# Norm of x, its two halves and beta times mask moved to earlier stages of the pass in a gated cross-attention and feed-forward kernel

## The chip, the cores and the metric

The kernel runs on one core of one Trainium2 chip. The metric is the time of one execution on the device, in microseconds. A core has five engines that run beside each other, each through its own list of instructions in order: TensorE (PE, with its weight loads as PEld), VectorE (DVE), ScalarE (ACT), GpSimd (POOL) and SyncE (SP), which here issues DMA transfers. They meet only at semaphores.

## The reference

Sixteen batch elements of x (256 channels x 1024 positions) pass a cross-attention layer and a feed-forward layer. Cut to what matters:

```python
x = x + tanh(g_xattn) * xattn(layernorm(x), ctx, mask, mask_cond, wq, bq, wk, bk, wv, bv, wo, bo, gamma, beta)
x = x + tanh(g_ffn) * ffn(layernorm(x), w1, w3, w2, wr)

def xattn(x, y, mask, mask_cond, ...):          # conv: weights standardised by row, then einsum, + bias, * mask
    q, k, v = conv(y, wq, bq, mask_cond), conv(y, wk, bk, mask_cond), conv(x, wv, bv, mask)   # 8 heads of 32
    scores = softmax(q @ k.T / SCALE)                                # 32 x 32 per head
    out = conv(scores @ v, wo, bo, mask) + x
    out = normalise out over the channels * gamma + beta
    return out * mask

def ffn(x, w1, w3, w2, wr):                      # tokens are the rows of x, 1024 wide
    gates = top-2 softmax gates of x @ wr.T over 8 experts
    h = silu(silu(x @ w1.T) @ w3.T) @ w2.T
    out[expert index] += gate * h                # scatter to the first 8 rows
```

## The kernel before

The kernel takes the batch elements in 8 pairs. Pass j works through the feed-forward layer of pair j and, threaded into it, the attention of pair j + 1. Seven passes carry an attention part: pass 0, which also still lays out the weights w3, and six steady ones. A pass has 16 groups of TensorE work (`GROUPS`), 24 matmuls of 512 columns each; during group g every engine also does stage s = g - 1 of the attention of the next pair. In each group ScalarE takes a tanh from PSUM (L894), VectorE multiplies (L1318), ScalarE makes the f16 high half (L900) and VectorE the low half (L1323). TensorE uses two PSUM banks in turn for this, so group g + 2 waits for L1318 of group g.

"First" and "second" are the two elements of a pair (b = 0 and 1). The stages of the attention, with the lines of the profile:

- stages 0 to 3: projections `project` (L531), evacuated by VectorE's `qk_out` (L1268) and scaled by ScalarE (L840); `scores` (L542) in stages 1 and 3, `softmax` by VectorE (L1183 to L1197) with ScalarE's exponential (L845).
- stages 3 to 5: `out_times_scores` (L554), split by `t1_high` (L856) and `t1_low` (L1273); `times_value` (L571, L576), split by `m_high` (L849) and `m_low` (L1176); ScalarE writes `cb` (L852). The second `out_times_scores` waits for the first `cb`, whose bank it overwrites.
- the norm of x: statistics `ln1` on VectorE (L1161, L1167), coefficients on GpSimd (L348 to L360), `normed` on ScalarE (L790, x scaled by 1024), the high half `x_high` on VectorE (L1172), the low half `x_low` on GpSimd (L375).
- `bias_part` on GpSimd (L410) writes bias times mask to `u`; `bias_tiles` on VectorE (L1206, eight tiles) adds `cb` times mask to it and signals `ub_ready`.
- stages 7 and 8: `long_product` (L591, L595), eight tiles t, which needs both halves of x. VectorE's `attention_out` (L1221, L1225, statistics L1216) takes the tiles up. There are four banks, so from its fifth tile on TensorE waits for L1225 of the tile three back.
- `values` on GpSimd gives the coefficients of the second normalisation (L348 to L360 on `coc`), ScalarE applies them (`v_normed`, L862), and TensorE transposes back in stages 9 and 10 (`attention_back`, L608).
- `add_beta` on GpSimd: beta times mask to `mtmp` (L391), added to x in place (L394), two pairs of instructions a call, four calls a pair of elements, each instruction behind the one before by the semaphore `mtmp_step`.

The order of work is written out by hand: `attention` and `attention_late` of each engine say what stands in which stage. In a group ScalarE and VectorE do the stage's `attention` first, then their part of the feed-forward; ScalarE does `attention_late` behind it.

Of the kernel before, what the change touches and what calls it, by code (L numbers as in the profile page):

```python
# [68 lines left out]
def build(nc, a, out):  # L69
    ctx = ExitStack()  # L70

    def sb(name, shape, dt=F32):
        return ctx.enter_context(nc.sbuf_tensor(name, shape, dt))
# [20 lines left out]
    with ctx:  # L94
# [66 lines left out]
        co = sb("co", [P, 4, 2])  # L161
# [58 lines left out]
        sm = {n: sem(n) for n in names}  # L220
# [106 lines left out]
        def _(pool):  # L327
# [40 lines left out]
            def ln1(q):  # L368
                coefs(q, mv, co, CH, EPS, XS, "ln1", (sm["xs_ready"], q))

            def x_low(q, b):
                pool.wait_ge(sm["xhi_ready"], q + 1)
                for h in range(4):
                    n, at = h // 2, slice(TC * (h % 2), TC * (h % 2) + TC)
                    ins = pool.tensor_tensor(x_lo[:, b, n, at], xs[b][:, n, at], x_hi[:, b, n, at], ALU.subtract)  # L375
                ins.then_inc(sm["xlo_ready"], 1)

            def add_beta(j, b, c):

                q = 2 * j + b  # L380

                for n in (2 * c, 2 * c + 1):
                    h = slice(TC * (n % 2), TC * (n % 2) + TC)
                    if n == 0:
                        pool.wait_ge(mrow_in[b], 16 * (j + 1))
                        pool.wait_ge(sm["xs_ready"], q + 1)
                        pool.wait_ge(sm["gcol_set"], 1)
                        need(pool, sm["xpre_ready"], q)
                    else:
                        pool.wait_ge(sm["mtmp_step"], 7 * q + 2 * n)  # L390
                    pool.tensor_tensor(mtmp[:, :], mrow[:, b, h], gcol[:, 1, c:c + 1].broadcast_to([P, TC]), ALU.mult)\  # L391
                        .then_inc(sm["mtmp_step"], 1)
                    pool.wait_ge(sm["mtmp_step"], 7 * q + 2 * n + 1)
                    pool.tensor_tensor(xa[b][:, c, h], xa[b][:, c, h], mtmp[:, :], ALU.add)\  # L394
                        .then_inc(sm["mtmp_step" if n < 3 else "xpre_ready"], 1)

            def values(q, b):

                coefs(q, mvc, coc, TT, EPS * XS * XS, 1.0, "cn", (sm["v_ready"], TT * q), m1c[:, b, :])
# [5 lines left out]
            def bias_part(q, b):  # L405

                pool.wait_ge(sm["sm_copy"], q + 1)
                for h in range(4):
                    tt = slice(2 * h, 2 * h + 2)
                    ins = pool.tensor_tensor(u[b][:, tt, :], bo_b[:, :].unsqueeze(1).broadcast_to([P, 2, S]),  # L410
                                             m1c[:, b, tt].unsqueeze(2).broadcast_to([P, 2, S]), ALU.mult)
                ins.then_inc(sm["ub_part"], 1)

            def attention(j, s, jn=None):
                if s == 12 and jn is not None:
                    y_largest(jn)
                if s in (3, 4):
                    ln1(2 * j + s - 3)
                if s in (2, 3):
                    bias_part(2 * j + s - 2, s - 2)  # L420
                if s in (5, 6):
                    x_low(2 * j + s - 5, s - 5)
                if s == 7:
                    add_beta(j, 0, 0)
                    values(2 * j, 0)
                    add_beta(j, 0, 1)
                    add_beta(j, 1, 0)
                if s == 8:
                    values(2 * j + 1, 1)
                    add_beta(j, 1, 1)  # L430
                if s in (9, 10):
                    second_norm(2 * j + s - 9)

# [352 lines left out]
        def _(act):  # L786
            def normed(q, b, c_, s_coef, s_done):
                act.wait_ge(s_coef, q + 1)
                for c in range(CH):
                    ins = act.activation(xs[b][:, c, :], xa[b][:, c, :], ACT.Identity,  # L790
                                         bias=c_[:, 3, c:c + 1], scale=c_[:, 2, c:c + 1])
                ins.then_inc(s_done, 1)
# [91 lines left out]
            def attention_late(j, s, jn=None):  # L884

                if s in (13, 14) and jn is not None:
                    y_high(jn, s - 13)
                if s in (4, 5):
                    normed(2 * j + s - 4, s - 4, co, sm["ln1_coef"], sm["xs_ready"])

            def ffn(j, g):
                first = g < FT
# [110 lines left out]
        def _(dve):  # L1003
# [152 lines left out]
            def ln1(j, b):  # L1156
                q = 2 * j + b
                dve.wait_ge(x_in[b], 16 * (j + 1))
                need(dve, sm[("ln2_mv", "ln1_mv")[b]], q)
                for n in range(4):  # L1160
                    ins = dve.bn_stats(bst[:, n, :], xa[b][:, n // 2, TC * (n % 2):TC * (n % 2) + TC])  # L1161
                ins.then_inc(sm["ln1_stat"], 1)
                dve.wait_ge(sm["ln1_stat"], q + 1)
                need(dve, sm["ln1_coef"], q)
                carry()
                for c in range(CH):
                    ins = dve.bn_aggr(mv[:, c, :], bst[:, 2 * c:2 * c + 2, :])  # L1167
                ins.then_inc(sm["ln1_mv"], 1)

            def x_high(q, b):  # L1170
                dve.wait_ge(sm["xs_ready"], q + 1)
                dve.tensor_copy(x_hi[:, b], xs[b]).then_inc(sm["xhi_ready"], 1)  # L1172
# [93 lines left out]
            def qk_out(q, b, t):  # L1266
                dve.wait_ge(sm["qk_mm"], CT * q + t + 1)
                dve.scalar_tensor_tensor(out=qk[b][:, t, :], in0=att[t][:, :], scalar=ysc[:, 2, b:b + 1],  # L1268
                                         in1=qkb_b[:, :], op0=ALU.mult, op1=ALU.add).then_inc(sm["qk_evac"], 1)
# [11 lines left out]
            def attention(j, s):  # L1281
                if s in (0, 2):
                    for t in range(CT):
                        qk_out(2 * j + s // 2, s // 2, t)
                if s in (1, 3):
                    softmax(2 * j + s // 2, s // 2)
                if s == 4:
                    m_low(2 * j, 0)
                if s in (3, 4):
                    t1_low(2 * j + s - 3)  # L1290
                    ln1(j, s - 3)
                if s in (5, 6):
                    bias_tiles(2 * j + s - 5, s - 5)
                    x_high(2 * j + s - 5, s - 5)
                if s == 5:
                    m_low(2 * j + 1, 1)
                if s in (7, 8):
                    attention_out(2 * j + s - 7, s - 7)
                if s in (9, 10):
                    residual(2 * j + s - 9, s - 9)  # L1300
                if s in (11, 12):
                    tokens_low(2 * j + s - 11, s - 11)
# [213 lines left out]
```

## Time and profile before

| | us |
|---|---|
| median of 3 runs (lowest, highest) | 1165.01 (1164.57, 1166.37) |
| profiled execution, its own time | 1164.77 |
| its span in the trace | 1163.0 |
| TensorE busy | 1056.6 (91%) |
| VectorE busy | 806.0 (69%) |
| ScalarE busy | 466.8 (40%) |
| GpSimd busy | 415.6 (36%) |

A "busy" figure is the time in which the engine has at least one instruction in work. Matmuls overlap, so 91% says that TensorE has something to do, and its idle time is what a program can lose there. The steady passes are 127.47 us apart. Positions in the span are in microseconds from its start.

### The profile page before, as it was taken

Reading aid. Unit: us, or ns where it says so; the run is one execution under the profiler, and the core shown is the slowest. Engines: PE = TensorE matmul, PEld = TensorE weight load, DVE = VectorE, ACT = ScalarE, POOL = GpSimd, SP = SyncE. Lnnn points to the kernel's source line nnn. Section 1 sums busy time; section 2 is a strip of 40 time slices with the busy share of each in tenths; the row PEclk is TensorE's granted clock in tenths of the full one; section 3 lists DMA queues with packets and bytes.
Section 4 is the critical chain, followed back from the end, with each engine's and each line's share of the span. In section 5 each row is a group of like instructions: output and inputs, shape, how many; then the busy total and the mean of one; then the engine's idle time right before and its main releaser. Section 6 shows DMA issues by size and latency. Waiting matters only on the chain.

```text
span 1163.0 us, 17830 instructions
## 1 busy us (share of the span) xinstructions
PE 1056.6 (91%) x6627; PEld 608.0 (52%) x6627; DVE 806.0 (69%) x1913; ACT 466.8 (40%) x714; POOL 415.6 (36%) x500
## 2 busy tenths in 40 slices
PE   4566279899999999999999999999999999999998
PEld 2355145564556555564556555655556455654452
DVE  6787457896679747986689657975788658973221
ACT  4456333345242633354243533353234524262331
POOL 2472002481147403671158212750167114730000
PEclk9778589999999999999999999999999999999999
DMA  8801700017100540027001620035001700054000
GB/s 269 219 19 55 216 1 1 1 63 188 42 1 27 135 128 0 18 78 192 0 0 36 172 80 0 18 117 153 0 0 72 213 4 0 0 142 149 1 1 2
DMA packets 102753, 81.82 MB, mean 70 GB/s; under 512 B 69342, under 2 KB 87332, under 8 KB 102716
## 3 DMA queue, kind: packets, MB, share of 16 engines
q1 hardware_dynamic: 100656, 79.77, 23.5%
q10 hardware_dynamic: 2060, 1.58, 0.5%
q8 instruction: 21, 0.34, 0.1%
q14 instruction: 16, 0.13, 0.0%
HBM read 47.75 MB, written 16.81 MB: 56 GB/s over the span
## 4 chain that ended last, share of the span: by engine, by line
PE 55%; DVE 23%; POOL 8%; issue 8%; ACT 5%; DMA 1%; ACTq 1%; POOLq 0%; DVEq 0%
PE bank L655 38%; PE bank L531 7%; DVE ub L1206 6%; DVE ub L1225 3%; DVE ub L1221 2%; PE bank L542 2%; POOL xbuf L394 2%; POOL mtmp L391 2%; POOL coc L355 2%; DVE bst L1161 2%; PE bank L554 1%; DVE bst L1216 1%; ACT h_hi L900 1%; DVE act_t L1318 1%; DVE x_hi L1172 1%
## 5 line engine op out<-in xcount | busy, mean ns | idle before, releaser
L655 PE MATMUL bank<-xt_hi,w1b 128*128 128x512 f16 x1024 | 326.7, 381 | 0.0
L655 PE MATMUL bank<-w3b,h_hi 128*128 128x512 f16 x1024 | 304.5, 379 | 0.5 <-DVE act_t L1318 0.5
L655 PE MATMUL bank<-xt_lo,w1b 128*128 128x512 f16 x512 | 194.9, 381 | 0.0
L655 PE MATMUL bank<-w3b,h_lo 128*128 128x512 f16 x512 | 194.0, 379 | 0.0
L894 ACT ACTIVATE act_t<-bank,fs 128x512 f32<-128x512 f32 x128 | 87.1, 680 | 193.8 <-PE bank L655 193.7
L1323 DVE SCALAR_TENSOR_TENSOR h_lo<-act_t,h_hi 128x512 f16<-128x512 f32 x128 | 98.4, 769 | 91.7 <-ACT h_hi L900 91.7
L900 ACT ACTIVATE h_hi<-act_t 128x512 f16<-128x512 f32 x128 | 80.8, 632 | 199.2 <-DVE act_t L1318 199.2
L655 PEld LDWEIGHTS bank<-xt_hi,w1b 128*128 128x128 f16 x1024 | 100.6, 98 | 114.3 <-issue 2.1
L1318 DVE SCALAR_TENSOR_TENSOR act_t<-act_t,bank 128x512 f32<-128x512 f32 x128 | 86.2, 673 | 102.0 <-ACT act_t L894 101.8
L655 PEld LDWEIGHTS bank<-w3b,h_hi 128*128 128x128 f16 x1024 | 98.0, 98 | 76.6 <-DVE act_t L1318 0.5
L410 POOL TENSOR_TENSOR ub<-bo_b,mcur 128x512 f32<-128x512 f32 x64 | 64.6, 1039 | 163.8 <-DVE dg L1183 163.8
L348 POOL TENSOR_TENSOR co<-mv,minus 128x2 f32<-128x2 f32 x32 | 7.2, 226 | 243.5 <-DVE mv L1167 153.5
L375 POOL TENSOR_TENSOR x_lo<-xbuf,x_hi 128x512 f16<-128x512 f32 x64 | 80.4, 1288 | 36.6 <-DVE x_hi L1172 31.8
L531 PE MATMUL bank<-wqk_hi,x_hi 128*128 128x512 f16 x256 | 86.9, 384 | 0.8 <-ACT wo_t L806 0.7
L790 ACT ACTIVATE xbuf<-xbuf,co 128x1024 f32<-128x1024 f32 x64 | 75.8, 1232 | 23.3 <-POOL co L360 23.2
L394 POOL TENSOR_TENSOR xbuf<-xbuf,mtmp 128x512 f32<-128x512 f32 x64 | 81.5, 1273 | 5.0
L655 PEld LDWEIGHTS bank<-w3b,h_lo 128*128 128x128 f16 x512 | 50.0, 98 | 60.4
L655 PEld LDWEIGHTS bank<-xt_lo,w1b 128*128 128x128 f16 x512 | 50.3, 98 | 54.8 <-issue 0.8
L1268 DVE SCALAR_TENSOR_TENSOR ub<-bank,ysc,qkb_b 128x512 f32<-128x512 f32 x64 | 47.1, 748 | 45.6 <-PE bank L531 45.4
L862 ACT ACTIVATE ub<-ub,coc 128x256 f32<-128x256 f32 x128 | 64.8, 591 | 29.0 <-POOL coc L360 29.0
L595 PE MATMUL bank<-m_hi,x_hi 128*128 128x256 f16 x256 | 70.1, 274 | 0.0
L595 PE MATMUL bank<-m_hi,x_lo 128*128 128x256 f16 x256 | 70.1, 274 | 0.0
(200 smaller groups left out, 1814.6 us busy)
## 6 DMA issues: line engine op xcount, KB each, us to landing
xbuf<-in_x_dram SPq DMA_DIRECT2D x16, 1024.0 KB, 8.6
out_dram<-xbuf SPq DMA_DIRECT2D x16, 1024.0 KB, 4.2
x_lo<-in_ctx_dram SPq DMA_DIRECT2D x16, 512.0 KB, 3.5
mrow<-in_mask_dram SPq DMA_DIRECT2D x16, 512.0 KB, 4.3
w1b<-in_w_dram SPq DMA_DIRECT2D x8, 512.0 KB, 7.3
w3b<-in_w_dram SPq DMA_DIRECT2D x8, 512.0 KB, 7.7
xbuf<-in_w_dram SPq DMA_DIRECT2D x1, 4096.0 KB, 13.6
xt_hi<-x_hi SPq DMA_TRANSPOSE x32, 4.1
```

What stands on the lines that cost most here:

```text
L375: ins = pool.tensor_tensor(x_lo[:, b, n, at], xs[b][:, n, at], x_hi[:, b, n, at], ALU.subtract)
L394: pool.tensor_tensor(xa[b][:, c, h], xa[b][:, c, h], mtmp[:, :], ALU.add)\
L531: mm = pe.matmul(att[t][:, :], left[b][:, c, P * t:P * t + P], right[:, c, :], start=n == 0, stop=n == 5)
L595: mm = pe.matmul(bk[:, S:2 * S], left[:, b, c, P * t:P * t + P], right[:, b, c, :], start=n == 0, stop=n == 5)
L655: mm = pe.matmul(bk[:, :], left, right, start=d == 0 and n == 0, stop=d == FT - 1 and n == 2)
L790: ins = act.activation(xs[b][:, c, :], xa[b][:, c, :], ACT.Identity, bias=c_[:, 3, c:c + 1], scale=c_[:, 2, c:c + 1])
L862: act.activation(u[b][:, t, :], u[b][:, t, :], ACT.Identity, bias=coc[:, 3, t:t + 1], scale=coc[:, 2, t:t + 1]).then_inc(sm["v_ready"], 1)
L894: act.activation(act_t[:, g % 2, :], fbk[g % 2][:, :], ACT.Tanh, scale=fs[:, 0:1] if first else fs[:, 1:2]).then_inc(sm["th_ready"], 1)
L900: act.activation(h1_hi[:, g, :] if first else h2_hi[:, g % 3, :], act_t[:, g % 2, :], ACT.Copy, scale=H1S if first else H2S).then_inc(sm[" ...
L1206: ins = dve.scalar_tensor_tensor(out=u[b][:, t, :], in0=cb[:, b, :], scalar=m2c[:, b, t:t + 1], in1=u[b][:, t, :], op0=ALU.mult, op1=ALU.add)
L1318: dve.scalar_tensor_tensor(out=buf, in0=buf, scalar=1.0, in1=fbk[g % 2][:, :], op0=ALU.add, op1=ALU.mult)\
L1323: dve.scalar_tensor_tensor(out=lo, in0=buf, scalar=H1S if first else H2S, in1=hi, op0=ALU.mult, op1=ALU.subtract).then_inc(sm["h_lo"], 1)
```

## The change

All of it is in the order of the stages, for the pairs 1 to 7; no instruction is added or taken away, but two waits of GpSimd are new. In VectorE's list `ln1` moves from stages 3 and 4 to stages 1 and 2 and `x_high` from 5 and 6 to 3 and 4. ScalarE's `normed` moves from the end of stages 4 and 5 to the end of 2 and 3. On GpSimd the first `bias_part` waits for the end of the first softmax (`s_ready`), where it waited for its copy out of PSUM; `x_low` moves to stages 3 and 4 and the second `bias_part` between the two; all four `add_beta` calls come in stages 5 and 6, each pair of them behind `ub_ready` of its element, that is behind `bias_tiles`, and ahead of both `values`.

```diff
@@ gpsimd
             def attention(j, s, jn=None):
                 if s == 12 and jn is not None:
                     y_largest(jn)
-                if s in (3, 4):
-                    ln1(2 * j + s - 3)
-                if s in (2, 3):
-                    bias_part(2 * j + s - 2, s - 2)
+                if s == 2:
+                    pool.wait_ge(sm["s_ready"], 2 * j + 1)
+                    bias_part(2 * j, 0)
+                    ln1(2 * j)
+                if s == 3:
+                    ln1(2 * j + 1)
+                    x_low(2 * j, 0)
+                    bias_part(2 * j + 1, 1)
+                if s == 4:
+                    x_low(2 * j + 1, 1)
                 if s in (5, 6):
-                    x_low(2 * j + s - 5, s - 5)
-                if s == 7:
-                    add_beta(j, 0, 0)
-                    values(2 * j, 0)
-                    add_beta(j, 0, 1)
-                    add_beta(j, 1, 0)
-                if s == 8:
-                    values(2 * j + 1, 1)
-                    add_beta(j, 1, 1)
+                    pool.wait_ge(sm["ub_ready"], 2 * j + s - 4)
+                    add_beta(j, s - 5, 0)
+                    add_beta(j, s - 5, 1)
+                if s in (7, 8):
+                    values(2 * j + s - 7, s - 7)
@@ scalar, attention_late
-                if s in (4, 5):
-                    normed(2 * j + s - 4, s - 4, co, sm["ln1_coef"], sm["xs_ready"])
+                if s in (2, 3):
+                    normed(2 * j + s - 2, s - 2, co, sm["ln1_coef"], sm["xs_ready"])
@@ vector
             def attention(j, s):
                 if s in (0, 2):
                     for t in range(CT):
+                        if s == 2 and t == 2:
+                            ln1(j, 1)
                         qk_out(2 * j + s // 2, s // 2, t)
                 if s in (1, 3):
                     softmax(2 * j + s // 2, s // 2)
+                if s == 1:
+                    ln1(j, 0)
                 if s == 4:
                     m_low(2 * j, 0)
                 if s in (3, 4):
                     t1_low(2 * j + s - 3)
-                    ln1(j, s - 3)
+                    x_high(2 * j + s - 3, s - 3)
                 if s in (5, 6):
                     bias_tiles(2 * j + s - 5, s - 5)
-                    x_high(2 * j + s - 5, s - 5)
```

In the rows of the order a line number behind the change is up to two or five higher than before. On ScalarE the place is the start of stage 3 to the cb of stage 4, before the change (L845 exponential, L856 t1_high, L894 and L900 the feed-forward, L849 m_high, L852 cb, L856 the second t1_high):

```order
L845 ACTIVATE dg<-dg 128x64
L856 ACTIVATE t_hi<-bank 128x512
L893 REGISTER_ALU
L894 ACTIVATE act_t<-bank,fs 128x512
L900 ACTIVATE h_hi<-act_t 128x512
L849 ACTIVATE m_hi<-bank 128x512
L852 ACTIVATE cb<-bank,fs 128x256
L856 ACTIVATE t_hi<-bank 128x512
```

And the same place in the changed kernel:

```order
L847 ACTIVATE dg<-dg 128x64
L858 ACTIVATE t_hi<-bank 128x512
L895 REGISTER_ALU
L896 ACTIVATE act_t<-bank,fs 128x512
L902 ACTIVATE h_hi<-act_t 128x512
L792 ACTIVATE xbuf<-xbuf,co 128x1024 x2
L851 ACTIVATE m_hi<-bank 128x512
L854 ACTIVATE cb<-bank,fs 128x256
L858 ACTIVATE t_hi<-bank 128x512
```

The second `normed` now stands between the feed-forward's copy of group 4 and m_high and cb of stage 4; its two instructions stood behind group 5 before.

On GpSimd the place is the list from the first coefficients of a steady pass to the first beta work, as a difference (L410 bias_part, L348 to L360 coefficients, L375 x_low):

```order
-L407 REGISTER_ALU
-L410 TENSOR_TENSOR ub<-bo_b,mcur 128x512 x4
+L345 REGISTER_ALU
 L348 TENSOR_TENSOR co<-mv,minus 128x2
 L349 TENSOR_SCALAR co<-mv 128x2
 L353 TENSOR_TENSOR co<-co,nhalf 128x2
 L360 TENSOR_TENSOR co<-co 128x2
-L375 TENSOR_TENSOR x_lo<-xbuf,x_hi 128x512 x8
+L375 TENSOR_TENSOR x_lo<-xbuf,x_hi 128x512 x4
+L410 TENSOR_TENSOR ub<-bo_b,mcur 128x512 x4
+L375 TENSOR_TENSOR x_lo<-xbuf,x_hi 128x512 x4
```

The second bias_part has moved from in front of the second element's coefficients to between the two halves of x_low.

On VectorE the place is stage 5 to the first tile of attention_out, before (L1206 bias_tiles, L1172 the cast x_high, L1176 m_low):

```order
L1206 SCALAR_TENSOR_TENSOR ub<-cb,mcur,ub 128x256 x8
L1172 CAST x_hi<-xbuf 128x2048
L1176 SCALAR_TENSOR_TENSOR m_lo<-bank,m_hi 128x512
L1317 REGISTER_ALU
L1318 SCALAR_TENSOR_TENSOR act_t<-act_t,bank 128x512
L1323 SCALAR_TENSOR_TENSOR h_lo<-act_t,h_hi 128x512
L1206 SCALAR_TENSOR_TENSOR ub<-cb,mcur,ub 128x256 x8
L1172 CAST x_hi<-xbuf 128x2048
L1317 REGISTER_ALU
L1318 SCALAR_TENSOR_TENSOR act_t<-act_t,bank 128x512
L1323 SCALAR_TENSOR_TENSOR h_lo<-act_t,h_hi 128x512
```

And in the changed kernel:

```order
L1208 SCALAR_TENSOR_TENSOR ub<-cb,mcur,ub 128x256 x8
L1178 SCALAR_TENSOR_TENSOR m_lo<-bank,m_hi 128x512
L1322 REGISTER_ALU
L1323 SCALAR_TENSOR_TENSOR act_t<-act_t,bank 128x512
L1328 SCALAR_TENSOR_TENSOR h_lo<-act_t,h_hi 128x512
L1208 SCALAR_TENSOR_TENSOR ub<-cb,mcur,ub 128x256 x8
L1322 REGISTER_ALU
L1323 SCALAR_TENSOR_TENSOR act_t<-act_t,bank 128x512
L1328 SCALAR_TENSOR_TENSOR h_lo<-act_t,h_hi 128x512
```

Both casts have left this stretch; the rest stands as before.

## Rows read from the trace of the kernel before

**Rows 1.** The page: TensorE's granted clock in tenths of full, 40 slices.

```profile
PEclk9778589999999999999999999999999999999999
```

**Rows 2.** TensorE's waits, 300 to 1100 us: total, times, longest.

```profile
PE bank L591 <- DVE ub L1225: 7.5, 6, 1.2
PE bank L608 <- ACT ub L862: 6.5, 6, 1.1
PE bank L591 <- POOL x_lo L375: 5.0, 6, 0.8
```

**Rows 3.** Timeline of TensorE: start, duration, operation, count, idle before and releaser.

```profile
588.62 1.10 PE L554 MATMUL bank<-wo_t,sblk 128*128 128x256 f32 x4
...
613.02 0.44 PE L591 MATMUL bank<-ident,xbuf 128*128 128x128 f32 x2 [1.24 <-DVE ub L1225]
```

**Rows 4.** Timeline of VectorE, the same pass.

```profile
564.93 2.45 DVE L1197 TENSOR_TENSOR sblk<-dg,dr 32x64 f32<-32x64 f32 x4
...
582.09 0.91 DVE L1197 TENSOR_TENSOR sblk<-dg,dr 32x64 f32<-32x64 f32 x4
...
583.63 2.46 DVE L1161 BATCH_NORM_STATS2 bst<-xbuf 128x6 f32<-128x512 f32 x4
...
595.63 3.25 DVE L1206 SCALAR_TENSOR_TENSOR ub<-cb,mcur,ub 128x256 f32<-128x256 f32 x8
...
603.03 5.05 DVE L1206 SCALAR_TENSOR_TENSOR ub<-cb,mcur,ub 128x256 f32<-128x256 f32 x8
608.00 1.22 DVE L1172 CAST x_hi<-xbuf 128x2048 f16<-128x2048 f32 x1
...
610.51 1.60 DVE L1323 SCALAR_TENSOR_TENSOR h_lo<-act_t,h_hi 128x512 f16<-128x512 f32 x1 [0.70 <-ACT h_hi L900]
612.04 0.41 DVE L1221 TENSOR_TENSOR ub<-ub,bank 128x256 f32<-128x256 f32 x1
...
632.62 0.54 DVE L1232 BATCH_NORM_AGGREGATE mvc<-bst 128x2 f32<-128x6 f32 x7
```

**Rows 5.** Timeline of ScalarE, the same pass.

```profile
588.01 0.47 ACT L852 ACTIVATE cb<-bank,fs 128x256 f32<-128x256 f32 x1
...
594.90 2.36 ACT L790 ACTIVATE xbuf<-xbuf,co 128x1024 f32<-128x1024 f32 x2
...
637.52 4.05 ACT L862 ACTIVATE ub<-ub,coc 128x256 f32<-128x256 f32 x8 [3.12 <-POOL coc L360]
```

**Rows 6.** Timeline of GpSimd, the same pass.

```profile
609.30 4.95 POOL L375 TENSOR_TENSOR x_lo<-xbuf,x_hi 128x512 f16<-128x512 f32 x4 [3.87 <-DVE x_hi L1172]
614.21 1.03 POOL L391 TENSOR_TENSOR mtmp<-mrow,gcol 128x512 f32<-128x512 f32 x1
615.32 1.28 POOL L394 TENSOR_TENSOR xbuf<-xbuf,mtmp 128x512 f32<-128x512 f32 x1
...
634.20 0.21 POOL L348 TENSOR_TENSOR coc<-mvc,minus 128x8 f32<-128x8 f32 x1
```

**Rows 7.** Timelines of VectorE and GpSimd in the prologue.

```profile
59.91 6.06 DVE L1206 SCALAR_TENSOR_TENSOR ub<-cb,mcur,ub 128x256 f32<-128x256 f32 x6
...
60.36 5.33 POOL L375 TENSOR_TENSOR x_lo<-xbuf,x_hi 128x512 f16<-128x512 f32 x4 [4.73 <-ACT x_hi L938]
65.65 1.22 POOL L391 TENSOR_TENSOR mtmp<-mrow,gcol 128x512 f32<-128x512 f32 x1
```

**Rows 8.** TensorE by windows: length, busy time (count), granted clock, DMA share, GB/s.

```profile
49.20:53.00 3.80, 0.02 (x1) 1.00 0.21 51
53.00:55.80 2.80, 0.03 (x1) 0.50 0.00 0
...
151.80:155.40 3.60, 3.60 (x13) 0.50 0.00 0
```

**Rows 9.** The load of x: SyncE's timeline, and the page's us to landing.

```profile
539.51 0.89 SPq L255 DMA_DIRECT2D xbuf<-in_x_dram  x2
...
xbuf<-in_x_dram SPq DMA_DIRECT2D x16, 1024.0 KB, 8.6
```

## The prediction

> **What bounds the kernel now.** I read the page first, then the waits of TensorE, then each engine's timeline over one steady pass, last the clock. The page has TensorE busy for 91% of the span, and its clock is full from the sixth of the 40 slices on [rows 1]. So what is lost later is idle time of TensorE alone. In the waits over the six steady passes three kinds are left [rows 2]: 7.5 us for DVE's tiles of the attention output (L1225), 6.5 us for ScalarE's L862, 5.0 us for GpSimd's low half of x (L375). The reader is to see that this is 19 us, about 3.2 us a pass (4.1 with the issue time around the waits, by the starts of the matmuls), and that no engine other than TensorE is full. I follow the pass that runs from 547.9 to 675.4 us; the others repeat it every 127.47 us. On its timeline TensorE waits 1.24 us up to 613.02 [rows 3], where the fifth tile of stage 7 needs the bank that VectorE's first tile frees; the wait for L862, 1.1 us [rows 2], ends at 639.72. Since DVE starts its first tile at 612.04 [rows 4] and TensorE follows 0.98 us later, **the start of these tiles, D, sets this place**: each microsecond on D is one on the pass.
>
> **Part 1: where D goes.** D is the end of a chain on DVE, and all that the change moves ends in it. Times are those of this pass.
>
> *The norm.* ln1 costs DVE 2.70 us (2.46 for four bn_stats [rows 4], and the aggregation), twice. The first stands now behind the first softmax, whose four products took 2.45 us beside the bias product of GpSimd and 0.91 us without it (the second softmax) [rows 4]; L1188 gains 0.7 too, so 2.2 of 2.7 us come back. The second stands between two evacuations of the second projection and makes the last ready 0.7 us later; the scores of TensorE then wait some 0.3 us. Both are absorbed by what follows. In stages 3 and 4 the norm's place is taken by the cast that makes the high half, 1.22 us. The x that the norm reads is issued at 539.5 and lands 8.6 us later [rows 9]; the norm starts at 565.2, so nothing waits there.
>
> *ScalarE.* The second normed (2.36 us for two L790 [rows 5]) comes now ahead of m_high and L852 in stage 4, before it came behind. ScalarE gets to it at 586.9, is free at 589.1, L852 ends at 590.1 where it ended at 588.48 (588.01 + 0.47 [rows 5]). The product out_times_scores of the second element waits for exactly this; it started at 588.62 [rows 3] and will at 590.2: TensorE is 1.6 us late from here on.
>
> *GpSimd.* x_low of the first element starts when DVE's cast ends, 585.7, and takes 4.95 us for four beside one DVE instruction [rows 6]. bias_part(1) follows from 590.7, is held up by the second cast (1.22 us [rows 4]) and ends at about 595.7. x_low(1) then runs to about 601, which lies over the first bias_tiles of DVE; before it had GpSimd idle beside it, 3.25 us for eight [rows 4].
>
> *How DVE and GpSimd hold each other up.* In the prologue six L1206 take 6.06 us with four L375 beside them [rows 7]: two pass at 0.40, four take 1.30 each, one for each GpSimd instruction. An L375 is 1.12 us without this ((4.95 - 0.45) / 4 [rows 6]), so a product costs GpSimd's instruction less some 0.2 us, plus its own 0.40. The reverse stands in the row of L391, 1.22 us where it has 1.03 alone [rows 6, 7]. In the pass it is seen again: eight L1206 in 5.05 us instead of 3.25, and L1323 in 1.60 instead of 0.69 [rows 4]. The Trainium skill (SBUF — State Buffer, "Who interferes with whom") says that DVE with two SBUF inputs contends with a GpSimd instruction that reads SBUF and that the loser blocks for the whole instruction. The rows agree with the first half and show some 0.2 us less than the second; by the page's wording the six slow products below would be 1.7 us dearer in each pass, by estimate 12 us in all, and I do not use it.
>
> *Sum on DVE.* L1323 of group 6 is issued at 596.0 and ends at 597.3. bias_tiles(0): three slow at 1.30, five at 0.40, 5.9 us, ends at 603.2. m_low(1) 0.6, L1318 0.6, ScalarE's copy 0.7, so the next L1323 is issued at 605.1. But add_beta of the first element begins at 603.2, since it waits for just this ub_ready. L1323 gets through at 606.1. bias_tiles(1) now meets the rest of the eight add_beta instructions, six of them: three L391 at 1.03 - 0.2 + 0.4 = 1.23 and three L394 at 1.28 - 0.2 + 0.4 = 1.48 [rows 6], 8.1 us, and two at 0.40: 8.9 us instead of 5.05, ends at 615.0 (before: 608.1). The cast behind it is gone (-1.14). L1318, the copy and an L1323 that meets the second add_beta take 1.9 to 2.85 us, middle 2.3. **D = 617.3 instead of 612.04: +5.3 us.** L391 and L394 beside several two-input DVE instructions are in no row. The bounds: no wait (0.40 a product) and a wait for every instruction in full, 1.03 or 1.28 and 0.48 for the product; I take the value of the nearest rows, L375's. TensorE is ready for the fifth tile at 612.2 (613.02, less the 1.24 and 1.0 us of waits with the issue time around them, 2.4 us, plus 1.6): it idles 6.1 us.
>
> **Part 2: what is won behind D.** GpSimd had the second coefficients' input at 633.16 but started at 634.20 [rows 4, 6], because the beta work lay in front. In the new order the beta work of both elements (19.8 us) ends at about 625.5, before the first statistics at D + 9.1 = 626.4, so neither element's values are delayed. L862 then starts about 1.2 us earlier (637.52 before [rows 5]), and TensorE's wait of 1.1 us [rows 2], 1.27 with the issue time, and the 0.19 behind it nearly go: -1.25 us. The x_low wait (1.0 us with issue) goes too, but it is inside the 6.1: VectorE's start is late next.
>
> **Part 3: the clock.** The stalls of the steady passes, 1.2 us at the longest [rows 2], leave it full [rows 1]. A stall of 6 us is of another kind: in the prologue TensorE idles from 49.22 to 55.77, and the clock is full for the first 3.8 us and at 0.50 (1.2 GHz of 2.4) after [rows 8]. After the idle time that ends at 151.77 TensorE works without gap, still at 0.50 for 3.6 us [rows 8], and from then on the clock stays full [rows 1]. I take this: 3.6 us at half speed lose 1.8 us. Bounds: 0, and 3.7 us as after 55.77, when the clock came back 7.5 us later, with gaps.
>
> **Sum.** A pass: +5.3 - 1.25 + 1.8 = +5.85 us. Seven passes carry an attention part that the change touches: six steady ones and the first, which has the same stalls plus the w3 weights; its stage 4 has more ScalarE work in front, so I give it the same. 7 x 5.85 = 41 us on the profiled execution's 1164.77 us (0.24 below the median): **1205.7 us**, and with the median 1206. I write 1205.5.
>
> **Rivals.**
> - *Faster: the products do not queue behind the beta work.* L394 is in place and L391 reads a broadcast column; if neither holds DVE, bias_tiles(1) ends at 609.0, D = 610.9, TensorE is at its fifth tile at 612.2 instead of 613.02, and with the 1.25 a pass is 2.05 us shorter: 1165 - 14.4 = 1150.6. It decides from D below 613.3 on. For it: no row has L394 against L1206. Against it: one L391 was lengthened by an L1206 [rows 7], and L410, which also reads a broadcast, held the softmax [rows 4].
> - *The clock holds.* Then +4.05 a pass, 1193.4. For it: TensorE is busy without gap up to the stall, where the prologue's work is thin, and the clock outlasted 3.8 us of idle time even there [rows 8]. Against: the stall forecast is 6.1 us.
> - *Two products to each beta instruction*, because GpSimd waits on its own semaphore between them. bias_tiles(1) ends at 613.0, D = 615.4, idle 4.2 us, +2.1 a pass: 1180, with the clock's loss 1192. Against: in the rows GpSimd gets the next turn each time; its gap between L391 and L394 is under 0.1 us.
> - *The norm does not come early*, because x or GpSimd is late: then about as before. The load's row [rows 9] excludes x.
>
> **Numbers.** The forecast 0.55; clock holds 0.17; two products 0.13; faster 0.09; about nothing 0.03; dearer than 1218 (the page's full block together with a slow return of the clock) 0.03. The range is 1177 to 1218; the likeliest alone has D from 616.8 to 617.8 and 0.9 to 3.1 for the clock, 1196 to 1218. What a measurement can tell from no change is 0.2%, 2.3 us: faster 0.09, same 0.03, slower 0.88.
>
> **What would show it.** The first L1221 of a steady pass some 5 us later in the pass; L1206 at a mean near 1 us (0.603 before), with a total near 15 us a pass for sixteen; TensorE's largest wait L591 for L1225, near 6 us, six times, and none for L375; L862's wait gone; out_times_scores 1.6 us late behind L852; a granted clock below 1.00 just after each long stall. Wrong it would be if bias_tiles(1) stayed near 5 us, if GpSimd were not in add_beta beside it, or if the fifth tile came less than 1.3 us later than before.

## The result, and the profile after

| | before | after |
|---|---|---|
| median of 4 runs, us (lowest, highest) | 1164.87 (1164.57, 1166.37) | 1207.27 (1206.68, 1208.89) |
| ratio to before, with its 95% interval | | 1.0364 [1.0346, 1.0381] |
| profiled execution, its span | 1163.0 | 1205.2 |

The changed kernel is 3.6% slower: the forecast of 1205.5 us is 1.8 us below the median. In the trace a line of before stands two to five lines higher: L1208 is `bias_tiles`, L1328 the feed-forward's low half, L1223 and L1227 the first and third operation of an attention tile, L593 the transposes of `long_product`, L854 `cb`, L864 `v_normed`.

The page, with the clock in 40 slices and the costliest row of `bias_tiles` (busy us, mean ns):

```profile
PEclk9777699999998999899999999899999999899999
...
L1208 DVE SCALAR_TENSOR_TENSOR ub<-cb,mcur,ub 128x256 f32<-128x256 f32 x128 | 110.0, 928 | 0.0
```

The waits of TensorE between 300 and 1100 us (total, times, longest), which answer to [rows 2]:

```profile
PE bank L593 <- DVE ub L1227: 39.6, 6, 6.7
PE bank L556 <- ACT cb L854: 5.2, 6, 0.9
PE bank L544 <- ACT ub L842: 1.2, 6, 0.2
```

The wait for VectorE's tile has grown from 1.2 to 6.7 us a pass, the waits for x_lo and for L864 (then L862) are gone, one for `cb` has come. The clock, full from the seventh slice on before [rows 1], now dips again and again.

I compare one pass with the pass of [rows 3 to 6]. Both are counted from their first matmul of `scores`, which is at 576.19 us here (first row below) and was at 560.03, so this pass stands 16.16 us later in the span. TensorE:

```profile
576.19 1.50 PE L544 MATMUL bank<-ub 128*128 128x128 f32 x12
...
606.34 1.10 PE L556 MATMUL bank<-wo_t,sblk 128*128 128x256 f32 x4 [0.86 <-ACT cb L854]
...
628.06 0.38 PE L657 MATMUL bank<-w3b,h_lo 128*128 128x512 f16 x1
635.09 0.69 PE L593 MATMUL bank<-ident,xbuf 128*128 128x128 f32 x2 [6.65 <-DVE ub L1227]
```

VectorE in the same pass, answering to [rows 4] (start, duration, operation, count, idle before):

```profile
612.17 1.33 DVE L1328 SCALAR_TENSOR_TENSOR h_lo<-act_t,h_hi 128x512 f16<-128x512 f32 x1 [0.70 <-ACT h_hi L902]
613.43 5.94 DVE L1208 SCALAR_TENSOR_TENSOR ub<-cb,mcur,ub 128x256 f32<-128x256 f32 x8
...
621.27 1.37 DVE L1328 SCALAR_TENSOR_TENSOR h_lo<-act_t,h_hi 128x512 f16<-128x512 f32 x1 [0.70 <-ACT h_hi L902]
622.55 8.62 DVE L1208 SCALAR_TENSOR_TENSOR ub<-cb,mcur,ub 128x256 f32<-128x256 f32 x8
631.10 0.68 DVE L1323 SCALAR_TENSOR_TENSOR act_t<-act_t,bank 128x512 f32<-128x512 f32 x1
632.47 1.71 DVE L1328 SCALAR_TENSOR_TENSOR h_lo<-act_t,h_hi 128x512 f16<-128x512 f32 x1 [0.70 <-ACT h_hi L902]
634.11 0.41 DVE L1223 TENSOR_TENSOR ub<-ub,bank 128x256 f32<-128x256 f32 x1
```

And GpSimd, answering to [rows 6]:

```profile
606.83 5.01 POOL L410 TENSOR_TENSOR ub<-bo_b,mcur 128x512 f32<-128x512 f32 x4
611.81 5.31 POOL L375 TENSOR_TENSOR x_lo<-xbuf,x_hi 128x512 f16<-128x512 f32 x4
619.69 1.04 POOL L391 TENSOR_TENSOR mtmp<-mrow,gcol 128x512 f32<-128x512 f32 x1 [2.58 <-DVE ub L1208]
620.81 1.27 POOL L394 TENSOR_TENSOR xbuf<-xbuf,mtmp 128x512 f32<-128x512 f32 x1
...
625.02 1.10 POOL L391 TENSOR_TENSOR mtmp<-mrow,gcol 128x512 f32<-128x512 f32 x1
626.20 1.33 POOL L394 TENSOR_TENSOR xbuf<-xbuf,mtmp 128x512 f32<-128x512 f32 x1
627.60 1.10 POOL L391 TENSOR_TENSOR mtmp<-mrow,gcol 128x512 f32<-128x512 f32 x1
628.78 1.32 POOL L394 TENSOR_TENSOR xbuf<-xbuf,mtmp 128x512 f32<-128x512 f32 x1
...
632.38 1.26 POOL L394 TENSOR_TENSOR xbuf<-xbuf,mtmp 128x512 f32<-128x512 f32 x1
```

Read these two lists side by side. VectorE's first group (613.43 to 619.37) lies over L375; its second (622.55 to 631.17) over the beta work that was released at 619.69; its last L1328 (632.47) over the next L394. Six of eight products in the second group each pay for one GpSimd instruction: from 625.02 on these start 1.18, 1.40 and 1.18 us apart, 1.29 on average for an L391 and an L394, and a held product takes 1.30. The price is nearly all VectorE's: in these rows L391 and L394 take 1.10 and 1.33 us, against 1.03 and 1.28 undisturbed [rows 6]. TensorE stood still from 628.44 to 635.09 meanwhile.

The clock around this stall (length, TensorE busy, granted clock):

```profile
628.40:635.10 6.70, 0.05 (x2) 0.70 0.00 0
635.10:637.90 2.80, 2.80 (x11) 0.50 0.00 0
637.90:641.00 3.10, 3.10 (x24) 0.99 0.00 0
```

TensorE resumes at half speed (1.2 of 2.4 GHz) and gets the full clock back at 637.9. It resumes so after each of the six long stalls; pass 0's stall, 3.65 us, left the clock full.

### The profile page after: what moved, and what is told of

Same layout as the page of the kernel before. It is cut to its first block, busy times and chain, and to the rows that moved or that the text cites. A ratio compares the mean times of both kernels' runs of the same rounds, so it can differ in the third digit from the quotient of the medians.

```text
span 1205.2 us, 17837 instructions
## 1 busy us (share of the span) xinstructions
PE 1069.1 (89%) x6627; PEld 612.7 (51%) x6627; DVE 848.1 (70%) x1913; ACT 467.1 (39%) x714; POOL 415.6 (34%) x500
## 4 chain that ended last, share of the span: by engine, by line
PE 55%; DVE 29%; ACT 8%; issue 7%; DMA 1%; ACTq 1%; POOL 0%; DVEq 0%; POOLq 0%
PE bank L657 36%; DVE ub L1208 9%; PE bank L597 5%; PE bank L533 4%; ACT xbuf L792 3%; DVE bst L1163 3%; DVE act_t L1323 2%; ACT h_hi L902 2%; PE bank L610 2%; PE bank L593 2%; DVE ub L1270 2%; PE bank L544 1%; DVE sblk L1199 1%; PE bank L719 1%; DVE ub L1227 1%
## 5 line engine op out<-in xcount | busy, mean ns | idle before, releaser
L657 PE MATMUL bank<-w3b,h_hi 128*128 128x512 f16 x1024 | 307.7, 382 | 0.5 <-DVE act_t L1323 0.5
L1328 DVE SCALAR_TENSOR_TENSOR h_lo<-act_t,h_hi 128x512 f16<-128x512 f32 x128 | 111.3, 870 | 91.6 <-ACT h_hi L902 91.6
L410 POOL TENSOR_TENSOR ub<-bo_b,mcur 128x512 f32<-128x512 f32 x64 | 70.5, 1131 | 179.6 <-DVE sblk L1199 174.3
L1208 DVE SCALAR_TENSOR_TENSOR ub<-cb,mcur,ub 128x256 f32<-128x256 f32 x128 | 110.0, 928 | 0.0
L593 PE MATMUL bank<-ident,xbuf 128*128 128x128 f32 x256 | 52.8, 290 | 44.5 <-DVE ub L1227 43.9
L375 POOL TENSOR_TENSOR x_lo<-xbuf,x_hi 128x512 f16<-128x512 f32 x64 | 81.4, 1303 | 21.0 <-DVE x_hi L1174 17.2
L394 POOL TENSOR_TENSOR xbuf<-xbuf,mtmp 128x512 f32<-128x512 f32 x64 | 82.4, 1288 | 5.0
L391 POOL TENSOR_TENSOR mtmp<-mrow,gcol 128x512 f32<-128x512 f32 x64 | 72.2, 1129 | 30.4 <-DVE ub L1208 26.7
L657 PEld LDWEIGHTS bank<-xt_lo,w1b 128*128 128x128 f16 x512 | 50.3, 98 | 54.8 <-issue 0.8
L593 PEld LDWEIGHTS bank<-ident,xbuf 128*128 128x128 f32 x256 | 36.9, 150 | 70.9 <-DVE ub L1227 47.9
L864 ACT ACTIVATE ub<-ub,coc 128x256 f32<-128x256 f32 x128 | 64.7, 590 | 20.7 <-POOL coc L360 20.7
```

The costliest lines, as they stand in the source:

```text
L593: pe.transpose(bk[:, P * c:P * c + P], xs[b][:, c, P * t:P * t + P], ident[:, :])
L657: mm = pe.matmul(bk[:, :], left, right, start=d == 0 and n == 0, stop=d == FT - 1 and n == 2)
L1208: ins = dve.scalar_tensor_tensor(out=u[b][:, t, :], in0=cb[:, b, :], scalar=m2c[:, b, t:t + 1], in1=u[b][:, t, :], op0=ALU.mult, op1=ALU.add)
L1328: dve.scalar_tensor_tensor(out=lo, in0=buf, scalar=H1S if first else H2S, in1=hi, op0=ALU.mult, op1=ALU.subtract).then_inc(sm["h_lo"], 1)
```

## The experiments

Each ratio is to the kernel before, measured beside it. "Gap" is TensorE's idle time before the fifth tile of `long_product`; "D" is the start of the first attention tile on VectorE, from the first matmul of `scores`. The mean time between the starts of steady passes, and D and the first and second group of `bias_tiles` in the third of them (the one whose rows are shown):

| kernel | us | ratio [95%] | steady pass | D | groups |
|---|---|---|---|---|---|
| before | 1164.9 | | 127.48 | 52.0 | 3.25, 5.05 |
| after | 1207.3 | 1.0364 | 133.98 | 57.9 | 5.94, 8.62 |
| beta_back | 1180.1 | 1.0128 [1.0111, 1.0145] | 130.03 | 54.4 | 9.54, 3.25 |
| beta_alone | 1214.5 | 1.0419 [1.0401, 1.0436] | 134.29 | 58.1 | 3.25, 10.43 |
| bias_wait | 1165.4 | 0.9999 [0.9990, 1.0009] | 127.47 | 52.0 | 3.25, 5.05 |
| halved | 1186.9 | 1.0185 [1.0168, 1.0202] | 130.97 | 54.8 | 5.94, 6.55 |
| kept_busy | 1226.4 | 1.0527 [1.0506, 1.0548] | 138.43 | 57.9 | 5.95, 8.63 |
| kept_busy2 | 1195.9 | 1.0272 [1.0254, 1.0290] | 131.98 | 57.9 | 5.95, 8.63 |
| cb_first | 1205.5 | 1.0355 [1.0337, 1.0373] | 133.12 | 57.7 | 6.84, 8.62 |
| beta_order | 1158.8 | 0.9945 [0.9929, 0.9962] | 126.21 | 52.0 | 3.25, 5.05 |
| beta_behind | 1150.4 | 0.9877 [0.9861, 0.9894] | 125.10 | 50.8 | 5.94, 3.25 |
| both | 1145.8 | 0.9837 [0.9821, 0.9853] | 124.68 | 50.6 | 6.84, 3.25 |

### beta_back: the changed kernel with the beta work where it was

```diff
-                if s in (5, 6):
-                    pool.wait_ge(sm["ub_ready"], 2 * j + s - 4)
-                    add_beta(j, s - 5, 0)
-                    add_beta(j, s - 5, 1)
-                if s in (7, 8):
-                    values(2 * j + s - 7, s - 7)
+                if s == 7:
+                    add_beta(j, 0, 0)
+                    values(2 * j, 0)
+                    add_beta(j, 0, 1)
+                    add_beta(j, 1, 0)
+                if s == 8:
+                    values(2 * j + 1, 1)
+                    add_beta(j, 1, 1)
```

> The changed kernel with add_beta and values back in stages 7 and 8 as before, all else as changed. If the beta work beside the second bias_tiles is what makes the changed kernel slower (my theory): bias_tiles(1) falls from 8.6 us to 3.3 to 4 us, the first L1221 tile stands near 611 to 612 us of the reference pass instead of 618, the long wait of TensorE for L1227 is under 1 us, the clock stays full, and the time is 1155 to 1163 us, below before. If the cause is the normed ahead of cb on ScalarE (TensorE 1.6 us late), or the norm's place in VectorE's list: most of the loss stays, above 1180 us.

Measured 1180.05 us: most of the loss is gone, and yet the expectation failed. The first `add_beta` has no wait in front; with `x_low` done early it starts beside the first group. VectorE and then GpSimd in the trace of this kernel (`bias_tiles` is L1210):

```profile
603.16 9.54 DVE L1210 SCALAR_TENSOR_TENSOR ub<-cb,mcur,ub 128x256 f32<-128x256 f32 x8
...
615.20 3.25 DVE L1210 SCALAR_TENSOR_TENSOR ub<-cb,mcur,ub 128x256 f32<-128x256 f32 x8
```

```profile
601.54 5.31 POOL L375 TENSOR_TENSOR x_lo<-xbuf,x_hi 128x512 f16<-128x512 f32 x4
606.80 1.22 POOL L391 TENSOR_TENSOR mtmp<-mrow,gcol 128x512 f32<-128x512 f32 x1
608.10 1.33 POOL L394 TENSOR_TENSOR xbuf<-xbuf,mtmp 128x512 f32<-128x512 f32 x1
```

The conflict has changed groups: 9.54 and 3.25 us in place of 5.94 and 8.62. It supports the mechanism and refutes what I took for "undone": the order in the list doesn't keep two engines apart, only a wait or the data does.

### beta_alone: the kernel before with only the beta work moved

```diff
-                if s == 7:
-                    add_beta(j, 0, 0)
-                    values(2 * j, 0)
...
+                if s in (5, 6):
+                    pool.wait_ge(sm["ub_ready"], 2 * j + s - 4)
+                    add_beta(j, s - 5, 0)
+                    add_beta(j, s - 5, 1)
+                if s in (7, 8):
+                    values(2 * j + s - 7, s - 7)
```

> The kernel before with only the beta work and values moved (stages 5 and 6 behind ub_ready, values in 7 and 8). My theory: this part alone brings most of the loss, 1200 to 1225 us, with a wait for L1225 of 5 us or more in each pass and a lowered clock behind it. If the loss needs the earlier norm and the x_low beside the first bias_tiles: 1165 to 1185 us.

Measured 1214.47 us. The longest wait of its TensorE (here L589 is the transposes, L1223 the third operation of a tile):

```profile
PE bank L589 <- DVE ub L1223: 44.1, 6, 7.4
```

This part by itself loses more than the whole change does. Here x_low of the first element still runs when the second group starts, so all eight products are held, two by L375 and six by the beta work: 10.43 us, 8 x 1.30. The slowdown is its work. Of the 7 us more than the changed kernel's, some 2 are in the steady passes and 4.8 in pass 0 (142.7 against 137.9 us), where the clock fell twice.

### bias_wait: the kernel before with only the new wait for the softmax

```diff
+                if s == 2:
+                    pool.wait_ge(sm["s_ready"], 2 * j + 1)
```

> The kernel before with only the first bias product behind the softmax (the wait for s_ready). The softmax of stage 1 takes 3.1 us instead of 5.4. My theory: it is off the path, 1163 to 1166 us, within 0.2% of before. A rival, that VectorE's time in stage 1 counts: 2 us a pass, 1150 us.

Measured 1165.39 us, ratio 0.9999. The softmax did become shorter, 3.1 us instead of 5.4, and the time did not: this wait is off the path.

### halved: the changed kernel with beta instructions of half the length

```diff
-                    pool.tensor_tensor(mtmp[:, :], mrow[:, b, h], gcol[...], ALU.mult)
+                    for m in range(2):   # at, to: 256 columns each
+                        ins = pool.tensor_tensor(mtmp[:, to], mrow[:, b, at], gcol[...], ALU.mult)
...                                          # and the same for the addition to xa
```

> The changed kernel with each of add_beta's two GpSimd instructions per column half (the scalar product and the product with the mask, 512 columns each) cut into two of 256 columns, so that GpSimd does the same work in twice as many instructions. Theory: beside add_beta each two-input VectorE product of bias_tiles waits for one GpSimd instruction, whatever its length; instructions of half the length then hold a product of bias_tiles(1) to some 0.75 to 0.85 us in place of 1.18 and 1.41, its group takes about 6.4 us in place of 8.6, the fifth u tile comes about 2 us earlier and TensorE is idle about 4.4 us before it: 1185 to 1200 us. Rival: a product waits by the total time that GpSimd is at work, so the group keeps its 8.6 us and the kernel its 1207.

Measured 1186.90 us, and this is the sharpest of the tests: GpSimd does the same work in more instructions, and the kernel is 20 us faster than the changed one. Its VectorE (L1213 is `bias_tiles`), then its GpSimd:

```profile
615.36 6.55 DVE L1213 SCALAR_TENSOR_TENSOR ub<-cb,mcur,ub 128x256 f32<-128x256 f32 x8
...
623.20 1.10 DVE L1333 SCALAR_TENSOR_TENSOR h_lo<-act_t,h_hi 128x512 f16<-128x512 f32 x1 [0.70 <-ACT h_hi L907]
```

```profile
616.10 1.43 POOL L393 TENSOR_TENSOR mtmp<-mrow,gcol 128x256 f32<-128x256 f32 x2
617.61 1.65 POOL L399 TENSOR_TENSOR xbuf<-xbuf,mtmp 128x256 f32<-128x256 f32 x2
```

Eight products in 6.55 us are 0.82 us each, and GpSimd passes four instructions from 616.10 to 619.34, 0.81 each: one for one, as with the long ones, where six products take 1.30 us each ((8.62 - 2 x 0.40) / 6). What a product waits for is one instruction of the other engine, whatever its length. D is 3.1 us earlier, the gap 3.6 us instead of 6.7; the clock fell to half after it in the six steady passes too.

### kept_busy and kept_busy2: what the lowered clock costs

In both, the changed kernel's TensorE works through the stall; the products are read by nothing.

```diff
+                if t == 4 and b == 0 and not first_pair(q):
+                    for _ in range(28):      # kept_busy2: range(9), ident and qkb_b, f32
+                        pe.matmul(rbk[:, P:4 * P], wqk_hi[:, 0, 0:P], wqk_hi[:, 0, 0:3 * P], ...)
```

> The changed kernel with 28 added matmuls of 384 columns into an unused part of a bank, issued just ahead of the fifth tile's wait in stage 7 (4.5 us of work inside the idle time of 6.65 us; their result is read by nothing). If the clock's fall behind the long stall costs 1.8 us a pass: granted clock 1.00 all through the passes and 1207 - 6 x 1.8 = 1196 us (1193 to 1199). If the lowered clock costs nothing, because something else sets the time behind the stall: 1207 us. If TensorE's own work were short of time: above 1207.

Measured 1226.37 us, inconclusive on the clock. With the 28 extra products TensorE stopped at the start of five of the passes, 3.3 to 3.9 us each time. Waits of its TensorE, then the queue that carries instructions on its page:

```profile
PE bank L661 <- issue: 18.2, 5, 3.9
```

```profile
q8 instruction: 66, 1.08, 0.4%
```

66 transfers of instructions instead of the 21 on the changed kernel's page, 45 more or nine for each stop. I read this as code that is fetched again because TensorE's program became too long; the profile names the queue, not what the transfers carry. The second version fills the time with fewer instructions.

> The changed kernel with 9 added float32 matmuls of 384 columns (5.9 us of work, read by nothing) ahead of the fifth tile's wait; the 28 of kept_busy made TensorE's loop so long that its code was fetched anew in each pass (66 fetches instead of 21, 3.7 us idle at the loop's start). With 9, if the code stays: 21 fetches, the clock at 1.00 in the passes, and half of 2.85 us saved in each: 1207 - 8.6 = 1199 us. If the lowered clock costs nothing: 1207 us. If the code is fetched anew: 18 to 20 us above one of these.

Measured 1195.90 us, with 21 transfers and the clock full. Its TensorE by windows (length, busy, clock), to be held against the windows above (this pass stands 3.06 us earlier in the span, so its fifth tile starts at 632.03):

```profile
628.40:635.10 6.70, 5.85 (x31) 1.00 0.00 0
635.10:637.90 2.80, 2.80 (x22) 1.00 0.00 0
```

D and both groups are those of the changed kernel, and the fifth tile starts at the same place, 58.90. A pass is 131.98 us instead of 133.98 on average: **the lowered clock costs 2.0 us a pass**, and the stall itself the rest. Pass 0, where the added work is longer than the stall, was 1.5 us longer, so the whole gains 11.4 us and not 12. In single passes of the changed kernel it was 1.4 to 2.9 us (133.36 to 134.92). The longest is the one in which the clock stayed at half for all of this window of the changed kernel:

```profile
768.40:774.50 6.10, 6.06 (x23) 0.50 0.00 0
```

### cb_first: the second norm behind cb on ScalarE

```diff
                     m_high(2 * j + s - 4, s - 4)
+                if s == 4:
+                    normed(2 * j + 1, 1, co, sm["ln1_coef"], sm["xs_ready"])
...
-                if s in (2, 3):
-                    normed(2 * j + s - 2, s - 2, co, sm["ln1_coef"], sm["xs_ready"])
+                if s == 2:
+                    normed(2 * j, 0, co, sm["ln1_coef"], sm["xs_ready"])
```

> The changed kernel with the second normed between m_high with cb and the second t1_high in stage 4. TensorE's wait for cb falls from 0.9 us to under 0.2. My theory: D hangs on VectorE and GpSimd, and moves 0.9 us at most, so 1201 to 1207 us, with a longer idle time before the fifth tile. The rival, that the normed ahead of cb carries the loss: at least 1.2 us a pass less, 1197 us or below.

Measured 1205.45 us. The longest wait of its TensorE:

```profile
PE bank L593 <- DVE ub L1229: 44.9, 6, 7.5
```

The wait for `cb` is gone, and TensorE waits so much longer for VectorE, 7.5 us. TensorE's 1.6 us at `cb` were real and worth nothing there, because the fifth tile sets the time; D moved 0.2 us. A steady pass is 0.86 us shorter all the same, and the rest of that is the clock: it was full again 2.85 us after each stall, in the changed kernel 2.85 to 6.0 us after, 4.0 on average. Pass 0 gives 1.7 us of it back, since its stall grew from 3.65 to 5.23 us and the clock fell there too.

### beta_behind: the beta work behind the last product that it can hold up

```diff
-                if s in (5, 6):
-                    pool.wait_ge(sm["ub_ready"], 2 * j + s - 4)
-                    add_beta(j, s - 5, 0)
-                    add_beta(j, s - 5, 1)
-                if s in (7, 8):
-                    values(2 * j + s - 7, s - 7)
+                if s == 7:
+                    pool.wait_ge(sm["h_lo"], GROUPS * (j - 1) + 8)
+                    add_beta(j, 0, 0)
+                    add_beta(j, 0, 1)
+                    values(2 * j, 0)
+                    add_beta(j, 1, 0)
+                if s == 8:
+                    values(2 * j + 1, 1)
+                    add_beta(j, 1, 1)
```

> The changed kernel with the beta work behind both bias_tiles: it waits for the low half of group 7 (the last instruction ahead of the first tile of attention_out), then add_beta(0,0), add_beta(0,1), values of the first, add_beta(1,0), values of the second, add_beta(1,1). My theory (GpSimd beside bias_tiles is the loss): bias_tiles(1) 3.3 us, D near 611 of the reference pass, no wait for L1227 and none for the second v_normed, 2 us less a pass than before: 1151 us (1148 to 1156). If the earlier norm and the x_low beside the first bias_tiles cost by themselves: 1165 or more.

Measured 1150.43 us, faster than before. VectorE, then GpSimd (L1211 is `bias_tiles`, L1331 the low half, L1226 the first attention tile):

```profile
600.94 3.25 DVE L1211 SCALAR_TENSOR_TENSOR ub<-cb,mcur,ub 128x256 f32<-128x256 f32 x8
...
605.48 0.69 DVE L1331 SCALAR_TENSOR_TENSOR h_lo<-act_t,h_hi 128x512 f16<-128x512 f32 x1 [0.70 <-ACT h_hi L905]
606.09 0.41 DVE L1226 TENSOR_TENSOR ub<-ub,bank 128x256 f32<-128x256 f32 x1
```

```profile
606.49 1.04 POOL L391 TENSOR_TENSOR mtmp<-mrow,gcol 128x512 f32<-128x512 f32 x1 [10.31 <-DVE h_lo L1331]
```

GpSimd stands idle for 10.31 us beside VectorE's second group, which takes 3.25 us, and the last low half takes 0.69 instead of 1.71. The attention tiles read PSUM and are not lengthened by the beta work (L1226 takes 0.41 us with it, at 606.94 for one, as without).

### beta_order: only the order of one beta call

```diff
                     add_beta(j, 0, 0)
+                    add_beta(j, 0, 1)
                     values(2 * j, 0)
-                    add_beta(j, 0, 1)
                     add_beta(j, 1, 0)
```

> The kernel before with one change of order on GpSimd: add_beta(0, 1) is issued ahead of the first values, all else where it was. Theory: the mask's product that the second values waited behind is then done earlier, the wait of TensorE for v_normed (1.25 us in each steady pass) goes, and the time is 1165 less 7 to 9, about 1157 us. The rest of the way to beta_behind's 1150 would then be the earlier norm's. Rival: what gains in beta_behind is the earlier norm and its halves alone, and this order gives 1165.

Measured 1158.82 us, a little above the expectation. The steady passes are 1.41 us shorter, the first of them 0.7 us. But pass 0 is 0.8 us longer, since the clock fell in it (last section), and it starts 0.9 us later. The rest of the way to beta_behind, 8 us by the two ratios, comes with the earlier norm and the wait that keeps the beta work out of its way, together; by itself no run has the norm's move with a gain (beta_back, without that wait, lost). Waits of TensorE in beta_order, then in beta_behind:

```profile
PE bank L591 <- DVE ub L1225: 7.4, 6, 1.2
PE bank L591 <- POOL x_lo L375: 5.0, 6, 0.8
```

```profile
PE bank L559 <- ACT cb L857: 5.1, 6, 0.9
PE bank L547 <- ACT ub L845: 1.2, 6, 0.2
```

12.4 us of waits give way to 6.3, 1.0 us a pass, as the passes say (126.07 behind the first one, and 125.10); pass 0 is 1.7 us shorter.

### both: beta_behind and cb_first together

> beta_behind and cb_first in one. With D no longer late, TensorE's 1.2 us behind cb count: 3 us less a pass than before, 1144 us (1140 to 1150). If only one of the two counts: as beta_behind, 1151 us.

Measured 1145.78 us, the fastest. The waits of its TensorE:

```profile
PE bank L596 <- DVE ub L1232: 2.7, 6, 0.5
PE bank L547 <- ACT ub L845: 1.2, 6, 0.2
```

Here the 1.6 us at `cb` do count, since D is no longer late. They give only 0.4 us a steady pass: `bias_tiles` starts 1.1 us earlier (36.1 instead of 37.2), lies over more of x_low and takes 6.84 us instead of 5.94.

## Why the prediction was right

Each step of the prediction beside the trace; positions are counted from the first matmul of `scores`.

| step | predicted | measured |
|---|---|---|
| second out_times_scores late | 1.6 | 1.56 (30.15 against 28.59) |
| first group: start, length | 37.3, 5.9 | 37.24, 5.94 |
| second group: start, length | 46.1, 8.9 | 46.36, 8.62 |
| end of second group to D | 2.3 | 2.93 |
| D | +5.3 | +5.90 |
| TensorE idle before the fifth tile | 6.1 | 6.65 |
| wait for v_normed | -1.25 | -1.41 |
| lowered clock | +1.8 | +2.0 |
| steady pass | +5.85 | +6.50 |
| pass 0 | +5.85 | +3.29 |

*The chain on VectorE.* It came as worked out, in its place and its count: three slow products in the first group, six in the second. beta_alone, beta_behind and halved each show that it is the beta work beside the second group, and that the price is one GpSimd instruction for a product. The rival "two products to each beta instruction" gave the second group 6.9 us and falls with the 8.62, and with halved, where GpSimd's instructions follow each other in twos without a semaphore and still hold one product each; "the products do not queue" is refuted by 8.62 us. The rival in which the norm is late falls with the rows of L375 and L1208: both lie where the sum put them.

*How large a price.* I took an instruction less 0.2 us plus 0.40. The rows give (8.62 - 0.80) / 6 = 1.30 us on average; my 1.23 and 1.48 had a mean of 1.36. The group was 0.3 us cheaper than forecast. GpSimd's own step from one start to the next, 1.29 us, would have been the better rule.

*The tail was mis-sized.* The last L1328 took 1.71 us and D came 2.93 us after the group, just outside the 1.9 to 2.85 of the forecast. ScalarE's copy put it at 632.47, right behind the start of a beta instruction at 632.38, so it waited for nearly all of it. This, and a start 0.3 us later because L1328 of the group before took 1.37 us, is why D is +5.90 instead of +5.3: +0.3 for the start, -0.3 for the group, +0.6 for the tail.

*Behind D.* -1.41 is the steady pass of kept_busy2 (127.48 + 5.91 - 1.41 = 131.98, its fifth tile being 5.91 us later than before). beta_order gives the same 1.41 alone. The forecast counted 1.25 of the 1.27 + 0.19 us there.

*The clock.* It fell in all six steady passes, so the rival "the clock holds" is out. The prediction has the clock full from the sixth slice on; [rows 1] shows an 8 there and the full clock from the seventh, which changes nothing for the steady passes. What it costs, 2.0 us, was forecast as 1.8 from the prologue's rows.

*Pass 0 was wrong.* I gave it the steady passes' sum. There `cb` came later still: ScalarE has the copies of w3 (L830) in front besides, and TensorE waited 2.01 us for it:

```profile
203.05 1.24 ACT L830 ACTIVATE w3b<-bank,sc 128x512 f16<-128x512 f32 x2
...
204.67 0.47 ACT L854 ACTIVATE cb<-bank,fs 128x256 f32<-128x256 f32 x1
```

VectorE was late there before too (D 58.34), and it got to its first group only at 43.17, when x_low was nearly done: 3.94 us instead of 5.94. D is +3.53, the stall 3.65 us, and the clock stayed full. Two errors cancelled: the passes cost 6 x 6.50 + 3.3 = 42.3 us, forecast 41, and the spans differ by 42.2. A steady pass was forecast 0.65 us too cheap and pass 0 2.6 us too dear. The mechanism was right; that the total came within 2 us is partly luck.

*The Trainium skill.* SBUF — State Buffer, "SBUF: two separate sides", has whichever instruction starts first hold the shared ports to its end and the other blocked. Here VectorE's rows stay somewhat under that: with L391 at 1.10 and L394 at 1.33 us, their mean and 0.40 for the product itself would be 1.62 us; measured were 1.30. GpSimd's rows stay far under it: a product of 0.40 us falls to each of its instructions, and they are 0.05 to 0.07 us longer than undisturbed. What the Trainium skill says of the pair of engines in the same page's "Who interferes with whom", two SBUF inputs on VectorE against a reader on GpSimd, the trace of each kernel here in which the two overlap bears out, the halves above all.

## What to carry to other kernels

The engines do not meet at semaphores alone. Free time of a helper engine is not free if the engine beside it contends with it: look what runs next to the new place, not only whether the place is empty. A two-input product there costs one instruction of the other engine (1.30 us instead of 0.40 here), so shorter instructions, or a wait that puts the work beside PSUM reads, are worth more than the idle time they leave. When part of a change is to be undone, check what kept the old place free of conflicts; in beta_back it was the late x_low, which no longer stood there.

## What the runs showed that I had not expected

The length of a stall alone doesn't decide whether the clock falls. Pass 0 of the kernel before, then of beta_order, both with TensorE idle for 1.7 us before the same matmul (windows: length, busy, clock):

```profile
220.50:222.20 1.70, 0.01 (x1) 1.00 0.00 0
222.50:229.00 6.50, 6.05 (x44) 1.00 0.01 3
```

```profile
221.40:223.10 1.70, 0.00 (x1) 0.79 0.00 0
223.20:229.20 6.00, 6.00 (x23) 0.50 0.01 3
```

The clock held in one and fell in the other. In beta_alone it fell behind the same stall of 1.74 us, in bias_wait it held. The difference need not be the kernel's: over the four executions of beta_order the mean granted clock was 0.965, 0.970, 0.965 and 0.969, with 1159.0, 1158.1, 1159.1 and 1158.7 us. Only the first has a trace, so it is not shown that the clock held in pass 0 of the others. In beta_back it fell after one of six stalls of 2.0 us, in halved after all six of 3.3 to 3.6 us, and not after the 3.65 us of pass 0 in the changed kernel. What else decides, these runs leave open.

The length of TensorE's program can be a cost of its own: 56 more instructions a pass (28 products with their weight loads) brought 3.3 to 3.9 us of idle time at the start of five passes. The nine f32 products of kept_busy2 stand in its trace as 18 matmuls with their weight loads, 36 instructions, and brought none.
